# Attention with a mixture of experts on one core: hidden sums split straight from PSUM, the first expert's weight work moved to later tiles, the scaled attention output written by ScalarE

## What is computed

```python
xn = layernorm(x)
# causal attention, one head of 256, with a linear bias
scores = (xn @ W_qk) @ xn.T / 16 + (kpos - qpos) * slope     # kpos <= qpos
s = softmax(scores) @ (xn @ W_v.T)
# mixture of 8 experts, top 1, capacity 4096 / 8 = 512 tokens each
probs = softmax(xn @ Wr);  e = argmax(probs);  p = max(probs)
ye = relu(xe @ W1[e]) @ W2[e] * p        # W1 256x1024, W2 1024x256
out = x + s * silu(y)                    # y: ye put back to its tokens
```

## Time and profile before

| | us |
|---|---|
| median of 3 runs (lowest, highest) | 486.47 (486.23, 486.49) |
| the profiled execution's own time | 486.67 |
| its span | 484.6 |
| PE busy | 441.1 (91%) |
| DVE busy | 343.6 (71%) |
| ACT busy | 251.5 (52%) |
| POOL busy | 223.0 (46%) |
| granted PE clock, mean | 0.98 of 2.4 GHz |

### The profile page before, as it was taken

How to read it: one execution, slowest core, us unless ns; L and a number is a source line. 1 busy time by engine, 2 the same in 40 slices (tenths; PEclk the granted TensorE clock), 3 DMA queues, 4 the chain that set the end, 5 groups by cost and what they waited for, 6 DMA issues and landing times.

```text
span 484.6 us, 8609 instructions
## 1 busy us (share of the span) xinstructions
PE 441.1 (91%) x3138; PEld 301.9 (62%) x3138; DVE 343.6 (71%) x881; ACT 251.5 (52%) x460; POOL 223.0 (46%) x337
## 2 busy tenths in 40 slices
PE   5777998999999989999999999999999999999960
PEld 2444575666677756767766787666666666666640
DVE  4779587687586757876765653889897979886340
ACT  1443452445544534444434344768686867768630
POOL 4107654333260373822040000257768787878761
PEclk9999998999999999999999999999999999999995
DMA  6982812603500485124002405347759475753140
GB/s 217 345 317 79 217 58 66 208 1 90 173 1 1 122 312 158 64 71 150 2 21 70 82 12 216 89 160 168 208 163 236 123 252 151 224 105 92 49 130 32
DMA packets 64313, 63.43 MB, mean 131 GB/s; under 512 B 36902, under 2 KB 58156, under 8 KB 62224
## 3 DMA queue, kind: packets, MB, share of 16 engines
q1 hardware_dynamic: 53472, 40.78, 29.4%
q0 software_dynamic: 5632, 16.73, 11.1%
q10 hardware_dynamic: 5168, 5.37, 3.4%
HBM read 30.29 MB, written 25.43 MB: 115 GB/s over the span
## 4 chain that ended last, share of the span: by engine, by line
PE 50%; DVE 29%; ACT 8%; issue 5%; POOL 3%; DMA 2%; SPq 1%; DVEq 0%; POOLq 0%; ACTq 0%
PE bank L1123 11%; PE bank L1125 11%; PE bank L1124 11%; DVE pmax L840 6%; DVE w_l L866 5%; PE bank L1194 4%; PE bank L1209 4%; PE bank L1212 4%; PE bank L1211 4%; DVE hid_l L884 3%; DVE sc L807 2%; DVE pT_l L823 2%; ACT hid_h L1049 1%; ACT sc L1026 1%; DMA sc<-in_w_r 1%
## 5 line engine op out<-in xcount | busy, mean ns | idle before, releaser
L1032 ACT ACTIVATE pT_h<-bank 128x512 f16<-128x512 f32 (+2 forms) x80 | 42.3, 530 | 82.9 <-PE bank L1194 82.7
L823 DVE SCALAR_TENSOR_TENSOR pT_l<-bank,pT_h 128x512 f16<-128x512 f32 (+2 forms) x80 | 48.6, 608 | 42.9 <-ACT pT_h L1032 41.6
L1209 PE MATMUL bank<-v_h,pT_h 128*128 128x257 f16 x272 | 75.0, 276 | 0.6 <-DVE pT_l L823 0.6
L1212 PE MATMUL bank<-v_h,pT_l 128*128 128x257 f16 x272 | 74.3, 273 | 0.0
L1211 PE MATMUL bank<-v_l,pT_h 128*128 128x256 f16 x272 | 74.0, 272 | 0.0
L1123 PE MATMUL bank<-w_h,hid_h 128*128 128x256 f16 x256 | 69.8, 273 | 2.7 <-DVE w_l L866 2.6
L884 DVE TENSOR_TENSOR hid_l<-hid,hid_h 128x512 f16<-128x512 f32 x64 | 49.6, 781 | 30.3 <-ACT hid_h L1049 30.1
L1125 PE MATMUL bank<-w_h,hid_l 128*128 128x256 f16 x256 | 69.8, 273 | 0.0
L1124 PE MATMUL bank<-w_l,hid_h 128*128 128x256 f16 x256 | 69.8, 273 | 0.0
L1123 PE MATMUL bank<-xT,qT_h 128*128 128x512 f16 (+3 forms) x160 | 56.0, 353 | 7.3 <-DVE cmin L807 5.8
L1026 ACT ACTIVATE sc<-sc,rmin 128x512 f32<-128x512 f32 (+2 forms) x72 | 43.3, 659 | 30.2 <-DVE rmin L814 30.2
(11 more groups left out here) (169 smaller groups left out, 953.4 us busy)
## 6 DMA issues: line engine op xcount, KB each, us to landing
raw<-in_w_e SPq DMA_DIRECT2D x5, 2048.0 KB, 9.1
sc<-in_w_e SPq DMA_DIRECT2D x3, 2048.0 KB, 7.6
slots<-empty ACTq DMA_DIRECT2D x1, 4224.0 KB, 26.1
out<-xg SPq DMA_DIRECT2D x8, 512.0 KB, 3.3
rows<-xg SPq DMA_DIRECT2D x8, 512.0 KB, 4.2
rows<-so SPq DMA_DIRECT2D x8, 512.0 KB, 3.0
xg<-in_x SPq DMA_DIRECT2D x6, 512.0 KB, 4.3
xg<-in_x ACTq DMA_DIRECT2D x2, 512.0 KB, 6.0
```

Of the source, the lines that this page charges most:

```text
L823: v.scalar_tensor_tensor(pT_l[:, t % 2, cols], tr_ps[n % 2][:, 0:w], P_UP, pT_h[:, t % 2, cols], ALU.mult, ALU.subtract).then_inc(pT_lo, 1)
L1209: pe.matmul(pv_ps[t % 2][:, 0:D + 1], pT_h[:, t % 2, rows_], v_h[:, at, q, 0:D + 1], start=kb == 0, stop=False)
L1212: last = pe.matmul(pv_ps[t % 2][:, 0:D + 1], pT_l[:, t % 2, rows_], v_h[:, at, q, 0:D + 1], start=False, stop=kb == t % NT)
```

## The change

1. **Hidden sums.** The scales are smaller (`X_UP` 2^2, and the experts' weights by `E_TOP` = 4 instead of 14 bits), so that relu of the raw sum fits into float16. ACT writes hid_h straight from the bank in one ACTIVATE; DVE writes hid_l = max(bank, 0) - hid_h in one scalar_tensor_tensor from the same bank. The buffer hid and the semaphore h_read are gone; an up product now waits for h_lo, the hid_l that last reads its bank.
2. **First expert's weight work.** FIRST_MAX goes from tiles 4 to 7 to tiles 8 to 11, FIRST_SCALE from 8 to 12, FIRST_SPLIT from 8 to 15 to 12 to 19. The second load goes from tile 16 to tile 20; its maxima stay.
3. **Output tile.** DVE makes only s_mul = rinv * value_mul (128x1); ACT writes so = bank * s_mul in one ACTIVATE, placed behind `high(t, c)` of the same step as DVE's `finish` and ahead of `probs(t + 1)`. The wait for the store of the buffer (rows_s) goes with it. The last tile's stands between the first two `hidden`.

```diff
--- before.py
+++ after.py
@@ -42,9 +42,10 @@
 PIECES = WCOLS // PIECE
 
 
-X_UP = 2.0 ** 10
-ACC_DOWN = 2.0 ** -18
+X_UP = 2.0 ** 2
+ACC_DOWN = 2.0 ** -8 / X_UP
 W_TOP = 14
+E_TOP = 4
 UNDO = 2.0 ** 8
 SM_SCALE = 2.0 ** -4
 P_UP = 2.0 ** 14
@@ -202,7 +204,6 @@
         pk = [sb(f"pk{k}", [P, SJ]) for k in range(2)]
         get_idx = [sb(f"get_idx{k}", [P, SJ], U32) for k in range(2)]
         put_idx = [sb(f"put_idx{k}", [P, SJ], U32) for k in range(2)]
-        hid = sb("hid", [P, 2, CAP])
         hid_h = sb("hid_h", [P, HB, CAP], F16)
         hid_l = sb("hid_l", [P, HB, CAP], F16)
         gate = sb("gate", [P, SJ, D])
@@ -338,8 +339,9 @@
             return late + [(g, n) for n in mine] + later
 
 
-        FIRST_MAX, FIRST_SCALE, FIRST_SPLIT = (4, 5, 6, 7), 8, tuple(range(8, 16))
+        FIRST_MAX, FIRST_SCALE, FIRST_SPLIT = (8, 9, 10, 11), 12, tuple(range(12, 20))
         SECOND_MAX = (22, 23, 24, 25, 26, 27, 28, 29)
+        SECOND_LOAD = 20
         FIRST_ROWS = TILES - 2
 
         def share(tiles, t):
@@ -445,7 +447,7 @@
                     turn(g + 2)
                 if t == FIRST_SCALE - 1:
                     spread(0)
-                if t == NT:
+                if t == SECOND_LOAD:
 
                     sp.wait_ge(w_lo, 2 * PIECES)
                     sp.dma_start(raw[:, :, :], w_k[1]).then_inc(w_in[1], 16)
@@ -711,13 +713,13 @@
             v.tensor_reduce(small_max[:, 2:3], wsmall[:, 2, :, 0:E], AX.XY, ALU.max, apply_absolute_value=True
                             ).then_inc(small_maxed, 1)
 
-            def scales(top, exp, up, dn):
+            def scales(top, exp, up, dn, bits=W_TOP):
 
                 step(v.tensor_scalar(exp, top, 2.0 ** -100, None, ALU.max))
                 step(v.tensor_scalar(exp.bitcast(I32), exp.bitcast(I32), 0x7F800000, None, ALU.bitwise_and))
-                step(v.tensor_scalar(up.bitcast(I32), exp.bitcast(I32), float((2 * 127 + W_TOP) << 23), -1.0,
+                step(v.tensor_scalar(up.bitcast(I32), exp.bitcast(I32), float((2 * 127 + bits) << 23), -1.0,
                                      ALU.subtract, ALU.mult))
-                step(v.tensor_scalar(dn.bitcast(I32), exp.bitcast(I32), float(W_TOP << 23), None, ALU.subtract))
+                step(v.tensor_scalar(dn.bitcast(I32), exp.bitcast(I32), float(bits << 23), None, ALU.subtract))
 
             norm_stats(1, range(GT))
             dve.wait_ge(consts_made, 8 + NX)
@@ -825,14 +827,11 @@
 
             def finish(t):
 
-                k, g = t % 2, t // GT
+                k = t % 2
                 dve.wait_ge(pv_full, t + 1)
                 step(v.reciprocal(rinv[:, k:k + 1], pv_ps[k][:, D:D + 1]))
-                if t % GT == 0 and g >= 2:
-
-                    dve.wait_ge(rows_s[g % 2], g // 2 * 16)
-                v.tensor_scalar(so[g % 2][:, t % GT, :], pv_ps[k][:, 0:D], rinv[:, k:k + 1], value_mul[:, 0:1],
-                                ALU.mult, ALU.mult).then_inc(s_made, 1)
+                v.tensor_scalar(s_mul[:, k:k + 1], rinv[:, k:k + 1], value_mul[:, 0:1], None, ALU.mult
+                                ).then_inc(s_mul_made, 1)
 
             def largest(buf, q):
 
@@ -853,11 +852,11 @@
                 if e < 2:
                     dve.wait_ge(w_spread, e * 16 + 16)
                     step(v.tensor_reduce(wtop[:, :], wall[:, :].rearrange("p (q m) -> p m q", m=2), AX.X, ALU.max))
-                    scales(wtop[:, :], wexp[:, :], wup[k][:, :], wdn[:, :])
+                    scales(wtop[:, :], wexp[:, :], wup[k][:, :], wdn[:, :], E_TOP)
                 else:
                     dve.wait_ge(w_told, e - 1)
-                    scales(w_back, wexp[:, :], wup[k][:, :], wdn[:, :])
-                v.tensor_scalar(ymul[k][:, :], wdn[:, 0:1], wdn[:, 1:2], UNDO, ALU.mult, ALU.mult
+                    scales(w_back, wexp[:, :], wup[k][:, :], wdn[:, :], E_TOP)
+                v.tensor_scalar(ymul[k][:, :], wdn[:, 0:1], wdn[:, 1:2], 1.0 / X_UP, ALU.mult, ALU.mult
                                 ).then_inc(w_scaled, 1)
 
             def split_low(buf, e, k, q):
@@ -881,8 +880,8 @@
             def hidden(m, f):
 
                 dve.wait_ge(h_hi, m + 1)
-                v.tensor_tensor(hid_l[:, f % HB, :], hid[:, f % 2, :], hid_h[:, f % HB, :], ALU.subtract
-                                ).then_inc(h_lo, 1)
+                v.scalar_tensor_tensor(hid_l[:, f % HB, :], sc_ps[f % 2][:, :], 0.0, hid_h[:, f % HB, :],
+                                       ALU.max, ALU.subtract).then_inc(h_lo, 1)
 
 
             split(0)
@@ -1032,21 +1031,26 @@
                 a_.activation(pT_h[:, t % 2, c * GTOK:c * GTOK + w], tr_ps[n % 2][:, 0:w], ACT.Copy, scale=P_UP
                               ).then_inc(pT_hi, 1)
 
+            def finish(t):
+
+                k, g = t % 2, t // GT
+                act.wait_ge(s_mul_made, t + 1)
+                if t % GT == 0 and g >= 2:
+
+                    act.wait_ge(rows_s[g % 2], g // 2 * 16)
+                a_.activation(so[g % 2][:, t % GT, :], pv_ps[k][:, 0:D], ACT.Copy, scale=s_mul[:, k:k + 1]
+                              ).then_inc(s_made, 1)
+
             def split_high(buf, e, k, q):
                 m, cols = piece(q)
                 act.wait_ge(w_scaled, e + 1)
                 a_.activation(w_h[k][:, m, cols], buf[:, m, cols], ACT.Copy, scale=wup[k][:, m:m + 1]
                               ).then_inc(w_hi, 1)
 
-            def hidden(m, f, first=False):
+            def hidden(m, f):
 
                 act.wait_ge(h_full, m + 1)
-                if not first:
-
-                    act.wait_ge(h_lo, m - 1)
-                a_.activation(hid[:, f % 2, :], sc_ps[f % 2][:, :], ACT.Relu, scale=ACC_DOWN).then_inc(h_read, 1)
-                act.wait_ge(h_read, m + 1)
-                a_.activation(hid_h[:, f % HB, :], hid[:, f % 2, :], ACT.Copy).then_inc(h_hi, 1)
+                a_.activation(hid_h[:, f % HB, :], sc_ps[f % 2][:, :], ACT.Relu).then_inc(h_hi, 1)
 
             def small_highs():
 
@@ -1080,6 +1084,8 @@
                     if c < chunks(t):
                         high(t, c)
 
+                    if c == chunks(t - 1) - 1:
+                        finish(t - 1)
                     ahead = min(chunks(t + 1), 2) if last_step(t, c) and (c or t % GT != 1) else 0
                     if ahead:
                         probs(t + 1, range(ahead))
@@ -1092,8 +1098,9 @@
 
             act.wait_ge(consts_made, 1)
             a_.activation(warm[:, :], empty[:, 0:1], ACT.Silu)
-            for f in range(LEAD):
-                hidden(f, f, True)
+            hidden(0, 0)
+            finish(TILES - 1)
+            hidden(1, 1)
 
             def expert(e):
                 k, o, more = e % 2, 1 - e % 2, e + 1 < E
@@ -1222,7 +1229,7 @@
                     pe.wait_ge(xeT_in[k], e // 2 * 16 + 16)
                 if not first:
 
-                    pe.wait_ge(h_read, e * NF + f - 1)
+                    pe.wait_ge(h_lo, e * NF + f - 1)
                 for d in range(KD):
                     cols = slice(d * F + f * P, d * F + (f + 1) * P)
                     last = product(sc_ps[f % 2][:, :], w_h[k][:, 0, cols], w_l[k][:, 0, cols],
```

3 lines of the change are left out of this document (2 added, 1 removed).

## The result

The changed kernel took **499.57 us** as the median of 4 runs (498.59 to 500.53); in the same set of runs the kernel before took 486.35. The ratio is 1.0253, 95% interval 1.0215 to 1.029: about 13 us slower. The forecast was 490.3, range 486.0 to 493.8. The direction is right and the size is not.

The account below looks back on a forecast made before the run. PE is busy 91%, its waits mostly released by DVE, with ACT heading each next tile's chain; -3.7 + 6.1 + 1.4 + 0 = +3.8 us on 486.67, forecast 490.3 against the median 486.47, range 486.0 to 493.8.

Parts of the forecast that it names:

- the price of the hidden sums: Experts: bank released by hid_l instead of the first relu, costed at nothing; the hidden sums save 3.7 us in all.
- The cover: Experts' up products: DVE, almost 1 us ahead, has some 0.5 us to spare before PE needs the bank.
- Rival 2: Experts: DVE does not get ahead, up waits for hid_l, 0.4 us per expert; experts give nothing, 494; chance 0.08.
- the lower bound: Experts' hid_l on DVE: reading the bank takes 0.1 us less per chunk; no change was taken.
- Output tile: Attention: ACT's tile waits for s_mul ahead of the next tile's exponentials, 0.77 us from the reciprocal's start; +6.1 us in sum.
- bound 0.47: ACT's output tile instruction: upper bound of its length by the gate's form; 380 ns was taken.
- Tile 15, said to be absorbed: Attention, tile 15: 0.6 us, absorbed by PE's wait for GpSimd's normed rows before 180.44.
- Rival 1: Attention: later waits absorb ACT's delay, only the DVE relief counts; about -6.5, 480, or 485 with half absorbed; chance 0.17.
- Weight work: Attention tiles 4 to 19: moving the first expert's weight work costs +1.4 us in sum.
- ACT's late split: Tile 6: DVE's 1.19 us relief meets ACT's split 0.8 us late, leaving -0.4 at PE's wait of 77.66.
- Clock: PE's clock stays up behind the wait of 77.66 (-1.6 us) and falls instead in tile 19 (+1.6): 0.

Follow-up runs that it names:

- hidden_weights: The changed kernel with the output tile put back on DVE, so hidden sums and weight work only; 480.96 us, ratio 0.9882.
- hidden_only: The kernel before with the hidden sums alone changed; 481.30 us, ratio 0.9893, and 480.75 us when run again.

## Why the prediction was right in direction and wrong in size

**The step that failed** is in the price of the hidden sums: "With DVE almost 1 us ahead it has some 0.5 us to spare ... I cost it at nothing; if that cover is gone it eats the gain". The cover holds only if hid_h starts when its product ends. In the profiled execution of the result chunk 7's starts 3 us late in six experts and 1.8 us in the seventh, because h_full rises late; the bank stays taken, and the experts cost +4.5 instead of -3.7: 8.2 us of the 9.3 between 490.3 and 499.6. Rival 2 named the right wait (up waits for hid_l) with another cause (hid_l running long) and so another price: it put the experts at zero gain, 494. Nothing in the profile of before shows such a lateness, and why the signal comes late is open. But the edit made PE depend within one chunk on two engines where it had depended on one; that exposure was visible, and the range had no term for it. PE's waits for hid_l (4.8 us in seven) show the bank as the path. How much of the 8.2 us came by it and how much by DVE's backlog was not separated, as nothing was late where a third bank was tried.

**The term itself was right on time.** Where nothing is late the experts gain 3.74 us (forecast 3.7) and the whole change costs +3.6 (forecast +3.8). The second agreement is partly luck, by the next two points. hid_l from the bank takes 684 to 685 ns: against the mean of 781 in the earlier trace rows it is a gain of 0.1 us, the lower bound, and against the undisturbed 680 no change. The Trainium skill ("VectorE: DVE Perf Modes", section on the TRN2 errata) would have an estimated 65 ns more per hid_l for the bank; the rows show none of it in this form.

**Output tile: place and mechanism right, size short, +9 to +11 in place of +6.1.** The answer to the earlier trace rows in the changed kernel (timeline of DVE, ACT, PE):

```profile
156.96 0.16 DVE L832 RECIPROCAL rinv<-bank 128x1 f32<-128x1 f32 x1
157.15 0.21 DVE L833 TENSOR_SCALAR s_mul<-rinv,value_mul 128x1 f32<-128x1 f32 x1
...
157.40 0.47 ACT L1041 ACTIVATE so<-bank,s_mul 128x256 f32<-128x256 f32 x1 [0.95 <-DVE s_mul L833]
157.77 1.32 ACT L1025 ACTIVATE sc<-sc,rmin 128x512 f32<-128x512 f32 x2
...
158.54 0.66 PE L1201 MATMUL bank<-ident,sc 128*128 128x128 f32 x4 [0.95 <-ACT sc L1025]
```

From the reciprocal's start to the exponential's 0.81 us (forecast 0.77), the tile 0.47 us long (I took 0.38, bound 0.47), PE's new wait 0.95 (forecast 1.0). Against hidden_weights tile 14 lost 1.4 us (1.3), tile 18 1.2 (1.1), tile 30 1.4 (1.3); tiles 1 to 4 together 1.8 to 2.4 (1.6), tiles 21 and 22 2.1 to 2.2 (1.4). Left out was that tiles 6 and 10, on which I put only the delay of ACT's split, stand behind the same wait: 1.15 and 1.25 us. Tile 15, said to be absorbed, cost 0.8. Tiles 9, 13, 25, 29 cost next to nothing, as said. Rival 1 fell: nowhere did a later wait absorb more than 1.0 us (tile 17).

**Weight work: sign wrong, -1.35 in place of +1.4.** Leaving tiles 6 and 8 gave 3.0 us where I put 1.2; 0.8 of the difference is that I charged ACT's late split to this part in tile 6, where it is the output tile's doing; the pmax that came to tiles 8 to 11 cost 0.4 in tile 9 and nothing in tile 10, where I had 0.6. The price at the new places was about right: +0.7 in tile 12 as forecast, 0.7 and 0.9 in tiles 16 and 19 for the +1.3.

So the agreement of +3.6 with +3.8 on time is two misses of about 3 us that cancel.

**Clock: both places as forecast, the price not.** Stretches with PEclk behind the five engines' busy times; first before, then after:

```profile
77.00:83.00 6.00, 5.34 (x25) 2.98 (x26) 4.25 (x13) 2.05 (x4) 4.07 (x13) 0.72 0.38 85
188.00:196.00 8.00, 8.00 (x57) 5.33 (x56) 4.96 (x18) 3.98 (x8) 5.43 (x14) 1.00 0.69 232
```

```profile
77.00:83.00 6.00, 5.13 (x39) 3.39 (x38) 4.12 (x15) 3.28 (x6) 3.05 (x12) 1.00 0.43 87
188.00:196.00 8.00, 6.71 (x38) 4.11 (x39) 4.97 (x19) 3.34 (x7) 3.02 (x12) 0.57 0.64 161
```

It no longer fell behind tile 6, and it fell in tile 19, for twice as long: 0.43 x 8 = 3.4 us of full-speed work missing against 0.28 x 6 = 1.7. That is up to +1.8 where I had 0. In time it is less, since PE waits in part of that stretch: the same attention program takes 268.9 us with this fall and 266.7 to 266.8 with none, +2.1, where before's fall in tile 7 costs 1.65 against hidden_only. Two things temper this. New waits of 0.6 to 1.3 us in tiles 15, 22 and 31 left the clock at 1.00, so it fell at one new place of four; the prediction had charged 1.6 us to each of them by the Trainium skill ("TensorE: Matmul & The Clock Gate", section on HAM oscillation). That section tells of waits for DMA that are several times longer, and these rows do not bear the charge out. And hidden_only had the same pair of waits in tile 6 as before, even longer (1.19 and 0.87), and kept its clock. Timeline of PE, then the stretch behind:

```profile
76.74 0.23 PE L1118 MATMUL bank<-xT,qT_h 128*128 128x128 f16 x1 [1.19 <-DVE cmin L807]
78.12 0.39 PE L1118 MATMUL bank<-xT,qT_h 128*128 128x512 f16 x1 [0.87 <-DVE cmin L807]
```

```profile
78.50:84.50 6.00, 6.00 (x47) 4.42 (x45) 4.64 (x14) 2.23 (x5) 3.93 (x11) 1.00 0.31 75
```

Where the clock falls varies between executions of one program; a term for one place is good to about 2 us.

## What to carry to other kernels

Work that waits for another engine must not stand ahead of what the next stage begins with, however short it is: the same 0.47 us ACTIVATE cost 9 to 11 us ahead of the exponentials and nothing behind them, and over half of that was the wait. When a buffer's release moves to a later consumer, add up how late each engine in that chain may be before the producer stands. Undo a change part by part, and run the whole of it again on another occasion, before believing what its profile accuses: here the profile pointed at a part that takes 3.7 us off the experts on time, and the experts came out 4.5 to 6.3 us longer than before only where the signals were late. When an engine starts late, look up when its semaphore rose, and whether the trace is complete.
